# Moving a convolution's middle row from VectorE to TensorE, reordering the stretch between two images, and widening two group norms' sums

## What is computed

```python
x = x + _L0_conv_ref(_gn(x), ...)     # layer 0
x = x + _L1_conv_ref(_gn(x), ...)     # layer 1
```

```python
wgt = filters.reshape(b * c, 1, k, k)
out = jax.lax.conv_general_dilated(x_r, wgt, window_strides=(1, 1),
          padding=[(pad, pad), (pad, pad)], feature_group_count=b * c, ...)
```

```python
dA = jnp.exp(delta[..., None] * A)
h = h * da + dbx ;  y = sum over the states of h * c
```

## Time and profile before

| | us |
|---|---|
| median of 3 runs | 4336.49 |
| range of the 3 runs | 4335.89 to 4338.08 |
| the profiled execution: its time | 4338.19 |
| the profiled execution: span of the instructions | 4336.4 |

### The profile page before, as it was taken

One profiled execution on the slowest core, in us unless ns is written; L12 is line 12 of the kernel. 1 busy time (PEld: TensorE's weight loads), 2 busy tenths in 40 slices (PEclk: granted clock), 3 DMA queues, 4 the chain that ended last, 5 costly groups with the idle time before them and its releaser, 6 DMA issues.

```text
span 4336.4 us, 51200 instructions
## 1 busy us (share of the span) xinstructions
PE 3086.1 (71%) x11852; PEld 1449.5 (33%) x11852; DVE 3559.6 (82%) x4199; ACT 2552.1 (59%) x6006; POOL 3338.1 (77%) x1908
## 2 busy tenths in 40 slices
PE   6977767777776778767777876777877777876511
PEld 3433333333332433333333333333333333332200
DVE  2178888888888888888888888888888888898777
ACT  4466665655665665666656666665676566565432
POOL 0069597895969879696896969789596996969798
PEclk8988788888888888887888888888887888888755
DMA  1036354463544446354453534446253454635444
GB/s 40 1 125 206 117 179 147 157 200 108 197 140 157 165 147 204 115 190 146 157 186 125 201 129 167 149 159 209 99 196 131 168 174 137 205 113 182 165 157 174
DMA packets 187260, 663.95 MB, mean 153 GB/s; under 512 B 22736, under 2 KB 24672, under 8 KB 186976
## 3 DMA queue, kind: packets, MB, share of 16 engines
q1 hardware_dynamic: 186976, 661.47, 45.0%
HBM read 639.76 MB, written 21.63 MB: 153 GB/s over the span
## 4 chain that ended last, share of the span: by engine, by line
POOL 28%; issue 23%; DVE 17%; PE 13%; ACT 11%; DMA 6%; DVEq 1%; POOLq 1%; SPq 0%; ACTq 0%
POOL bx L1342 12%; POOL y L1370 7%; DMA bb<-bc_rows 6%; DVE h L581 6%; POOL h L1365 5%; ACT diag L1085 5%; PE pconv L822 4%; DVE slot_c L572 3%; POOL bx L1345 2%; PE pm L848 2%; DVE rs L528 1%; DVE rs L520 1%; ACT slot_b L1200 1%; PE pm L839 1%; POOL delta L1310 1%
## 5 line engine op out<-in xcount | busy, mean ns | idle before, releaser
L822 PE MATMUL pconv<-pad,diag 128*128 128x512 f16 x8064 | 2052.6, 412 | 132.7 <-DVE xn L506 66.9
L1370 POOL TENSOR_TENSOR y<-y,h 128x1024 f32<-128x1024 f32 (+2 forms) x672 | 1335.6, 1987 | 153.9 <-DVE h L581 131.2
L1200 ACT ACTIVATE slot_b<-delta,nega 128x512 f32<-128x512 f32 (+1 forms) x1280 | 804.3, 640 | 1010.6 <-DVE slot_c L572 1009.0
L822 PEld LDWEIGHTS pconv<-pad,diag 128*128 128x128 f16 x8064 | 826.1, 104 | 1328.6 <-issue 423.3
L1342 POOL TENSOR_TENSOR bx<-bb,u 128x1024 f32<-128x1024 f32 x512 | 1219.4, 2382 | 19.9 <-DMA bb<-bc_rows 19.9
L572 DVE TENSOR_TENSOR_SCAN slot_c<-slot_b,bx 128x512 f32<-128x512 f32 (+1 forms) x1024 | 954.2, 956 | 296.1 <-POOL bx L1342 255.4
L581 DVE TENSOR_TENSOR h<-slot_c,cb 128x512 f32<-128x512 f32 x1280 | 860.4, 673 | 36.6 <-POOL y L1370 36.6
L572 DVE TENSOR_TENSOR_SCAN slot_c<-slot_b,slot_c,bx 128x512 f32<-128x512 f32 x512 | 663.7, 1296 | 74.8 <-ACT slot_b L1200 18.7
L1310 POOL TENSOR_TENSOR delta<-delta,rs 128x512 f32<-128x512 f32 (+1 forms) x96 | 111.8, 1164 | 464.6 <-DVE rs L530 464.6
L1365 POOL TENSOR_TENSOR h<-h 128x512 f32<-128x512 f32 (+3 forms) x384 | 361.2, 941 | 98.3 <-DVE h L551 80.7
L1085 ACT ACTIVATE diag<-id,chi 128x128 f16<-128x128 f16 x1344 | 426.6, 386 | 10.7 <-PE pconv L822 10.1
(11 more groups left out here) (168 smaller groups left out, 3555.2 us busy)
## 6 DMA issues: line engine op xcount, KB each, us to landing
bb<-bc_rows SPq DMA_DIRECT2D x592, 512.0 KB, 4.5
cb<-bc_rows SPq DMA_DIRECT2D x592, 512.0 KB, 4.4
xr<-in_x SPq DMA_DIRECT2D x16, 1024.0 KB, 4.9
out<-ob SPq DMA_DIRECT2D x16, 1024.0 KB
bc_rows<-rows SPq DMA_DIRECT2D x64, 64.0 KB, 1.6
w<-in_w SPq DMA_DIRECT2D x2, 256.0 KB
wc<-in_wc SPq DMA_DIRECT2D x2, 256.0 KB
bc_rows<-rows SPq DMA_DIRECT2D x16, 32.0 KB, 1.5
```

Of the source, the lines that this page charges most:

```text
L822: ins = nc.tensor.matmul(bank(pconv, k), w, pad[:, t, part, rows:rows + 16, dx:dx + W], start=first and m == 0, stop=last and m == 2)
L1200: ins = nc.scalar.activation(slot_b[:, o:o + w], delta[:, so + c:so + c + w], ACT.Exp, scale=nega[:, st, n0 + n:n0 + n + 1])
L1370: pool.tensor_tensor(yv, yv, src[:, 0] if len(src.shape) == 3 else src, ALU.add).then_inc(q_y.sem, 1)
```

## The change

There are four edits.

1. The middle row becomes two more rows of PE: `ROWS` has 14 entries, 98 taps. `middle_taps`, `wmid` and the tile `xm` are gone; `copy_x` copies `xr` itself. ACT makes 28 more diagonal matrices an image, `ROOM` stays as it is but for unit 15, and through `taps_at` and `row_unit` the taps and rows move in the units.
2. The bridge is reordered. DVE takes `chunk_last(j, 0)` before `norm(i, 4)`, and the two `scan_least` stand at its end and no longer in unit 0. ACT takes `chunk_log(j, 0)` between the two squares and the first decays before the copy of z. POOL does `inputs(j, 0)` before chunk 1; SP fetches the first rows before it writes those of chunk 1.
3. `copy_f(j, 0)` stands before the late half of the last unit's diagonal matrices, and only one tap instead of two stands on PE before `project_f`, two instead of one behind it.
4. `sums1` is one matmul of 8 columns instead of four of 2, `sums2` two instead of eight. The sum over the four moments of a channel half is made on ACT by the accumulator output: two instructions in `gn_spread` instead of one, two more and a wait in `gn_root`.

```diff
-MIDDLE = KK // 2
-ROWS = [(t, r) for t in range(CT) for r in range(KK) if r != MIDDLE]
+ROWS = [(t, r) for t in range(CT) for r in range(KK)]
...
             def bridge(i, j, m):          # SP
                     put_rows(j, 0)
-                    put_rows(j, 1)
...
-                    for k in range(2):
-                        get_b(j, k)
-                        get_c(j, k)
+                    get_b(j, 0)
+                    get_c(j, 0)
+                    put_rows(j, 1)
+                    get_b(j, 1)
+                    get_c(j, 1)
...
             def bridge(i, j, m):          # DVE
-                some(0, 1)
                 if j is not None:
                     chunk_first(j, 0)
-                some(1, 2)
+                if j is not None:
+                    chunk_last(j, 0)
                 if i is not None:
                     norm(i, 4)
...
                 if j is not None:
-                    chunk_last(j, 0)
                     chunk_last(j, 1)
-                some(2, 3)
                 if i is not None:
                     output(i, 0)
-                    some(3, 4)
                     output(i, 1)
-                else:
-                    some(3, 4)
-                some(4, 5)
                 if j is not None:
                     silu_clip(j)
+                    scan_least(j, 0)
+                    scan_least(j, 1)
...
             def sums1(b, s, pp, sums, stats):
-                for k in range(4):
-                    ins = nc.tensor.matmul(pp[:, 0:2], grp[:, :], moments(s)[:, :, k, 1], start=(k == 0), stop=(k == 3))
+                nc.tensor.matmul(pp[:, 0:8].rearrange("p (t k) -> p t k", t=CT), grp[:, :], moments(s)[:, :, :, 1],
+                                 start=True, stop=True).then_inc(sums.sem, 1)
...
             def gn_root(ch, b, s, pp, sums, total, var, rstd, shift):
-                nc.scalar.activation(s[:, 52:54], pp[:, 32:34], ACT.Ln, bias=eps[:, 0:1]).then_inc(var.sem, 1)
+                for t in range(CT):
+                    ins = nc.scalar.activation(s[:, 92 + 4 * t:96 + 4 * t], pp[:, 32 + 4 * t:36 + 4 * t], ACT.Copy,
+                                               accum_out=s[:, 100 + t:101 + t])
+                ins.then_inc(total.sem, 1)
+                act.wait_ge(total.sem, total.at(b, 1))
+                nc.scalar.activation(s[:, 52:54], s[:, 100:102], ACT.Ln, bias=eps[:, 0:1]).then_inc(var.sem, 1)
...
             def copy_x(j):
-                act.wait_ge(mid_tap.sem, mid_tap.at(j + 1, 0))
-                nc.scalar.activation(xn[:, :, :], xm[:, :, :], ACT.Copy).then_inc(a_copy.sem, 1)
+                nc.scalar.activation(xn[:, :, :], xr[:, :, :], ACT.Copy).then_inc(a_copy.sem, 1)
...
             def unit(i, j, m, k):         # ACT
                 if i is not None:
                     if 1 <= k < NU - 1:
                         decay(i, k + 1, 1)
+                if j is not None and k == PREP + 3:
+                    copy_f(j, 0)
                 row_parts(j, m, k, 1)
...
-BRIDGE_TAPS = (0, 2, 3, 3, 3, 3, 6, 9)
-BRIDGE_MID = (0, 7, 10, 11, 11, 14)
+BRIDGE_TAPS = (0, 1, 3, 3, 3, 3, 6, 9)
```

More of the change, by code:

```diff
@@ L730, in sums2 @@
                 d2 = s[:, 32:40].rearrange("p (t k) -> p t k", t=CT)
-                for k in range(4):
-                    nc.tensor.matmul(pp[:, 32:34], grp[:, :], d2[:, :, k], start=(k == 0), stop=False)
-                for k in range(4):
-                    ins = nc.tensor.matmul(pp[:, 32:34], grp_m2[:, :], moments(s)[:, :, k, 2], start=False, stop=(k == 3))
-                ins.then_inc(sums.sem, 1)
+                o = pp[:, 32:40].rearrange("p (t k) -> p t k", t=CT)
+                nc.tensor.matmul(o, grp[:, :], d2, start=True, stop=False)
+                nc.tensor.matmul(o, grp_m2[:, :], moments(s)[:, :, :, 2], start=False, stop=True).then_inc(sums.sem, 1)
             def a_key_(j):
@@ L1296, in unit @@
                         prep(m)
-                if j is not None and k == PREP + 3:
-                    copy_f(j, 0)
             stages(unit, bridge, act)
```

54 lines of the change are left out of this document (16 added, 38 removed).

## The result

The changed kernel takes 4222.8 us (median of 4 runs, 4222.1 to 4223.5) where the kernel before takes 4336.2: a ratio of 0.974, 95% interval 0.972 to 0.976. The profiled execution has a span of 4220.7 us (4336.4 before).

A forecast was written before the change was run, and what follows sets the result against it. The prediction took POOL's work plus the bridge and POOL's waits as the bound. An image's −4.4 us times 14 (−61.6), with +14.2, −4.8 and −3.3, made −55.5: 4281 us, with 8 in 10 within 4237 to 4332.

The forecast's parts named there:

- the clock in the bridge: PE in the bridge: more bridges run at 2.4 GHz instead of 1.2; −1.2 us an image, bounds 0 and −2.
- the middle: Units 5 to 10: PE waits for row 5's matrices and restarts slowly; +3.0 us an image, bounds 0 and +5.5.
- copy_f: ACT in the bridge: copying f1 ahead of eight diagonal matrices gives −2.3, accumulated sums +1.2; net −1.1 us an image.
- the end of the bridge: Output's end to chunk 2's first correction: starts earlier without DVE's middle taps; −5.1 us an image, bounds 0 and −6.8.
- First image and ends: Outside the loop's images: first image's convolution on PE +14.2 us, bridge behind it −4.8, bridge of the last image −3.3.
- (a): Middle of an image costs nothing: PE is fast on restart, or POOL's queue absorbs late scans; 4239 us, chance 0.20.
- (d): Slower: PE stays at 1.2 GHz through units 5 to 10, an image at +3.6; 4393 us, chance 0.11.

## Why the prediction was wrong in its size

The direction and the places were right, and so were most of the waits. What failed are sizes. Of the 60 us between the forecast for the spans (−55.5) and the measurement (−115.7) the clock in the bridge makes some 32, the middle 28 and the copy of f1 7; the end of the bridge and the ends of the run go the other way by some 6.

- **The clock in the bridge (−1.2, bounds 0 and −2).** This is the step that failed, since it lies beyond its bounds. It measured −3.5 (of the 5.1 up to the output's end, 1.6 is the copy of f1 that comes earlier). The prediction took the difference of 3.2 us between its two periods for all that a slow bridge had to win, and so put 2 on the mean as the most. So it took the bridge whose lowering was at 2.4 GHz for one that was at 2.4 throughout. But later groups in the same bridge were not; the lowering of the earlier trace rows at 2286.09 is followed there by

```profile
2290.68 1.30 PE L878 MATMUL slot_b<-y,cen 128*128 128x512 f32 x2
2291.77 1.91 PE L878 MATMUL slot_c<-y,cen 128*128 128x512 f32 x2
2293.62 1.06 PE L863 MATMUL pm<-f,wbc 128*32 128x256 f32 x2
```

  against 1.08, 1.02 and 0.62 after. Before, the output ended 53.0 us behind `conv_add` where the lowering took 3.78, 51.9 where it took 2.5 to 2.7, 49.3 in four of the five bridges where it took 2.01, and 47.7 in the fifth, which was at 2.4 GHz throughout; the mean is 51.4. Every bridge of the changed kernel but one is like this last, less 1.5. The prediction also named the tap as one of two causes; alone it gives no time, while the copy's place alone brings every lowering to 2.4 GHz. By the rule of the Trainium skill that the prediction weighed ("TensorE: Matmul & The Clock Gate", "What's actually happening": throttled by default, released by activity) every bridge would be at 2.4 GHz. After the change the trace agrees, with 2.01 us for all 16 lowerings; before it, with 3.78 us in seven of the loop's 14, it does not. And the same tap in another place changed nothing.
- **The middle (+3.0, bounds 0 and +5.5).** It measured +1.0, and only 0.4 of it where the prediction put 2.9, up to the first `conv_add`. PE was ready for ACT's root 9.6 us after row 5's matrices (2066.54 to 2076.18), not 11.4, since the 24 matmuls of taps took 6.41 us where the prediction has 8.0; and the two copies cost 0.45, not 0.7. That the price would be there without the wide sums is shown: with narrow ones the middle costs 4.1 us an image. The other 0.6 is a cost that the prediction did not name: chunk 4 of unit 13, whose matmuls take 1.2 us longer on the mean.
- **copy_f (−1.1).** −1.6: the order −2.3, the accumulating sums +0.7 and not +1.2, as the kernels with the copy alone (23.1 behind `conv_add`) and with all (23.8) show.
- **The end of the bridge (−5.1).** −4.8, and bound by ACT's chain of 17.4 us, as said. But the account of DVE's side was wrong. The prediction counted the taps' 5.6 us as gone and the branch as 1.23 us that the scans may hide. The row's move alone gives 0.7 us there, since the idle time at the branch grows from 1.1 to 5.2; only with the scans ahead of it does DVE come early enough for ACT to be last.
- **First image and ends.** +15.3 for +14.2, −5.4 for −4.8 and −2.1 for −3.3: right within the 3 us by which two profiles of the changed kernel differ there.
- **The rivals.** (a), 4239, was nearest. Its mechanism held for two of the middle's 3 us; the clock's part is not in it. (d) did not come: the 12 matmuls of taps behind the sums take 2.8 us again. That the row's move alone could cost time at the branch was not among the rivals: alone it is 94 us slower.

## What to carry to other kernels

A chain whose clock differs between repetitions may be at the lower one in parts of its shorter repetitions too: price the clock from the best repetition there is, link by link, and cure it at the engine that PE waits for. Work that stands ahead of a loop's branch may be hiding the branch; look at what the engine would do there before you count that work as won. When two waits end together, each edit alone shows nothing or a loss, and the pair must be judged together; and ask of work moved off a path which later step of the same engine it now stands in front of.
